# Graph units of an attention block: q/k parts written out and stacked through GpSimd's transfer queue instead of SyncE's

## The reference

```python
nodes = {-1: inputs}
for c in range(6):
    q = ew[c, 0] * (nodes[in_q] @ We[eq] + be[eq])
    k = ew[c, 1] * (nodes[in_k] @ We[ek] + be[ek])
    v = ew[c, 2] * (nodes[in_v] @ We[ev] + be[ev])
    o = _mha(q, k, v, Wq[c], Wk[c], Wv[c], Wo[c])     # 8 heads of width 16, softmax over 1024 keys
    nodes[c] = act_w[c] * o + q
out = layernorm(nodes[5], ln_g, ln_b)
x = x + out
```

## Time and profile before

| what | value |
|---|---|
| runs | 3316.85 us median, 3299.77 to 3317.97 |
| the profiled execution | 3333.32 us, of which the span is 3331.5 us |
| busy | TensorE 90%, VectorE 73%, ScalarE 65%, GpSimd 12% of the span |
| transfers | 245.09 MB, of them 239.85 MB on the queue of SyncE |
| granted clock of TensorE | 0.938 of full speed over the span |
| the graph stage | from about 883 us to about 3286 us |

### The profile page before, as it was taken

One profiled execution on the slowest core, in us unless ns is written; L12 is line 12 of the kernel. 1 busy time (PEld: TensorE's weight loads), 2 busy tenths in 40 slices (PEclk: granted clock), 3 DMA queues, 4 the chain that ended last, 5 costly groups with the idle time before them and its releaser, 6 DMA issues. The chain is left out here.

```text
span 3331.5 us, 49190 instructions
## 1 busy us (share of the span) xinstructions
PE 2998.8 (90%) x19007; PEld 1331.5 (40%) x19007; DVE 2418.4 (73%) x3094; ACT 2151.3 (65%) x2695; POOL 389.8 (12%) x330
## 2 busy tenths in 40 slices
PE   5699989989569999999999999999999999999994
PEld 4355555555323333333333333333333333333331
DVE  6656555554266688888888888888888888888853
ACT  1155555556313477777777777777777777777783
POOL 0000000000100011111111111111111111111114
PEclk9699999999755699999999999999999999999997
DMA  6000000000252244434444344434434444443302
GB/s 169 17 11 4 24 1 27 1 11 11 88 99 50 45 84 107 105 93 103 82 94 100 91 91 100 105 93 102 106 71 103 97 99 85 107 100 94 68 21 84
DMA packets 144224, 245.09 MB, mean 74 GB/s; under 512 B 56482, under 2 KB 92726, under 8 KB 140918
## 3 DMA queue, kind: packets, MB, share of 16 engines
q1 hardware_dynamic: 143414, 239.85, 32.2%
q10 hardware_dynamic: 576, 2.10, 0.2%
HBM read 165.00 MB, written 74.10 MB: 72 GB/s over the span
## 5 line engine op out<-in xcount | busy, mean ns | idle before, releaser
L1436 ACT ACTIVATE pt_b<-ps_max 128x1024 f32<-128x1024 f32 x1516 | 1493.1, 1024 | 436.1 <-PE ps_max L1287 431.8
L1469 DVE TENSOR_REDUCE mx_b<-ps_pair 128x2 f32<-128x1024 f32 (+1 forms) x1032 | 1245.6, 1207 | 243.9 <-PE ps_pair L1273 235.0
L1323 PE MATMUL ps_ctx<-pt_b,vs 128*32 128x512 f32 x6144 | 842.4, 621 | 3.8 <-ACT c_b L1425 3.5
L1469 DVE TENSOR_REDUCE mx_b<-ps_misc 128x1 f32<-128x512 f32 x1032 | 706.9, 685 | 163.9 <-PE ps_misc L1273 145.9
L1287 PE MATMUL ps_max<-qs,ks 50*128 50x512 f32 x3032 | 800.9, 443 | 3.6 <-DMA qs<-mpart 3.0
L1273 PE MATMUL ps_pair<-ks,qs 48*128 48x512 f32 x2040 | 557.7, 479 | 131.8 <-DVE mx_b L1469 104.2
L1287 PEld LDWEIGHTS ps_max<-qs,ks 50*128 50x128 f32 x3032 | 364.9, 190 | 341.0 <-ACT pt_b L1436 246.0
L1273 PE MATMUL ps_misc<-ks,qs 48*128 48x512 f32 x1032 | 482.2, 467 | 7.6 <-DVE mx_b L1469 0.6
L1273 PEld LDWEIGHTS ps_pair<-ks,qs 48*128 48x128 f32 x2040 | 226.9, 192 | 454.8 <-DVE mx_b L1469 395.2
L775 ACT ACTIVATE pt<-ps_max,cb 128x512 f32<-128x512 f32 x342 | 215.4, 684 | 236.0 <-PE ps_max L652 179.9
L1273 PEld LDWEIGHTS ps_misc<-ks,qs 48*128 48x128 f32 x1032 | 199.6, 193 | 360.9 <-DVE mx_b L1469 287.6
(11 more groups left out here) (181 smaller groups left out, 2382.6 us busy)
## 6 DMA issues: line engine op xcount, KB each, us to landing
partd<-part SPq DMA_DIRECT2D x24, 2048.0 KB, 9.1
qs<-partd SPq DMA_DIRECT2D x288, 128.0 KB, 5.7
ks<-partd SPq DMA_DIRECT2D x288, 128.0 KB, 6.7
xq<-node SPq DMA_DIRECT2D x24, 512.0 KB, 3.9
xk<-node SPq DMA_DIRECT2D x24, 512.0 KB, 4.8
xv<-node SPq DMA_DIRECT2D x24, 512.0 KB, 5.5
xf<-node SPq DMA_DIRECT2D x24, 512.0 KB, 4.7
node<-nt_b SPq DMA_DIRECT2D x48, 256.0 KB, 2.2
```

What stands on the lines that cost most here:

```text
L1323: ins = pe.matmul(psO[SLOT * i:SLOT * i + SLOT, :], vs[u % 2][:, kb, QUAD * (s // HALF_STEPS) + i], pt[:, (QUAD * S + i) % ENTRIES], start ...
L1436: act.activation(pt[:, e:e + 2].rearrange("p k n -> p (k n)"), at[:], ACT.Exp, scale=SCALE_B).then_inc(exp_done, 1)
L1469: nc.vector.tensor_reduce(mx2[:, at:at + n], (psP, psX)[p % 2][:, 0:CHUNK * n].rearrange("p (h n) -> p h n", h=n), AX.X, ALU.max).then_inc ...
```

## The change

`spill` and `stack` are moved from SyncE's program to GpSimd's, and are otherwise the same: the same waits, the same sources and destinations, the same 25 transfers for a unit. All other transfers stay with SyncE. In GpSimd's `unit(u)`, `stack(u+1, 1)` stands behind the first maxima split, `spill(u+2)` behind the last split of unit u + 2, and `stack(u+2, 0)` between `normalise(u, 0)` and the next maxima split. At the start, unit 0 is spilled and stacked before the parts of unit 1 are split.

```diff
@@ sync
-                def spill(w):
-                    sp.wait_ge(split_done, PJ * (w + 1))
-                    ...
-                    sp.dma_start(partd, part[:].bitcast(F32)).then_inc(spilled, D16)
-                def stack(w, q):
-                    ...
                     if u:
                         maxima_rows(u, 1)
                         rows_of(NG * u - 1)
-                    if u < LAST:
-                        stack(u + 1, 1)
                     if u:
                         spread(NG * u - 1)
                         store(u - 1, 0)
...
                     load_residual(u)
-                    if u < LAST - 1:
-                        spill(u + 2)
                     if u < LAST:
                         spread(NG * u)
                     if u < LAST:
                         rows_of(NG * u + 1)
-                    if u < LAST - 1:
-                        stack(u + 2, 0)
...
-                spill(0)
-                stack(0, 0)
-                stack(0, 1)
-                spill(1)
                 maxima_rows(0, 0)
-                stack(1, 0)
@@ gpsimd
+                def spill(w):
+
+                    pool.wait_ge(split_done, PJ * (w + 1))
+                    if w:
+                        pool.wait_ge(stacked[0], STACK * w)
+                        pool.wait_ge(stacked[1], STACK * w)
+                    pool.dma_start(partd, part[:].bitcast(F32)).then_inc(spilled, D16)
+
+                def stack(w, q):
+
+                    if w >= 2:
+                        pool.wait_ge(exp_done, exps(w - 2, NS // 2 * (q + 1)))
+                    pool.wait_ge(spilled, D16 * (w + 1))
+                    heads = slice(2 * q, 2 * q + 2)
+                    for t, (a, b) in enumerate(TERMS):
+                        for qk, dst, k in ((0, qs, a), (1, ks, b)):
+                            src = partd[:, qk, k].rearrange("(j r d) t -> r d j t", r=2, d=DV)
+                            for odd in range(2):
+                                at = P // 2 * odd + DV * t
+                                pool.dma_start(dst[w % 2][at:at + DV, heads, :].bitcast(F32),
+                                             src[odd][:, heads]).then_inc(stacked[q], D16)
...
                     if u:
                         split_maxima(u, 1)
+                    if u < LAST:
+                        stack(u + 1, 1)
                     if u < LAST - 1:
                         for n in range(PJ - 1):
                             split(u + 2, n)
...
                         split(u + 2, PJ - 1)
+                        spill(u + 2)
                     if not u:
                         split_maxima(0, 1)
                     normalise(u, 0)
+                    if u < LAST - 1:
+                        stack(u + 2, 0)
                     if u < LAST:
                         split_maxima(u + 1, 0)
...
-                for w in range(2):
-                    for n in range(PJ):
-                        split(w, n)
+                for n in range(PJ):
+                    split(0, n)
+                spill(0)
+                stack(0, 0)
+                stack(0, 1)
+                for n in range(PJ):
+                    split(1, n)
+                spill(1)
                 split_maxima(0, 0)
+                stack(1, 0)
```

More of the change, by code:

```diff
@@ L1127, in load_residual @@
                     sp.dma_start(xf[:], row(node, u)).then_inc(f_in, D16)
-                def spill(w):
-                    sp.wait_ge(split_done, PJ * (w + 1))
-                    if w:
-                        sp.wait_ge(stacked[0], STACK * w)
-                        sp.wait_ge(stacked[1], STACK * w)
-                    sp.dma_start(partd, part[:].bitcast(F32)).then_inc(spilled, D16)
-                def stack(w, q):
[L1139 to L1149, removed]
                 def maxima_rows(w, q):
```

## The result

The changed kernel takes 3643.43 us, the median of four runs (3584.0 to 3667.45), against 3308.31 us for the kernel before on the same occasions. The ratio is 1.0916, with a 95% interval of 1.0758 to 1.1074: 9% slower, where no change was forecast. The profiled execution of the changed kernel took 3650.4 us (3333.32 before), its span is 3648.6 us.

What follows compares the result with a forecast made beforehand. TensorE, busy 90% of the span, was taken as the bound. Only the graph's start gained, 2.3 us, the other terms 0: 3316.85 - 2.3 = 3314.5 us, range 3284 to 3346 us.

Steps and rivals of the forecast that it cites:

- p: Time one stacking transfer's issue holds GpSimd, taken as 1.1 us, between a low end of 0.42 and a high of 2.04.
- the threshold of 1.69 us: At each unit's start, the longest issue time per stacking transfer on GpSimd before the output has to wait.
- the second rival: GpSimd's issues wait for VectorE's running reductions, growing to 2.31 us each: 3486 us, chance 0.04.
- Term 2: Each unit's start: 12 issues delay GpSimd's first split half a microsecond, absorbed; inverses of group 3 land sooner; time 0.
- Term 3: Each unit's middle: GpSimd's stacking and spill delay the maxima split some us, still ahead of need; time 0.
- Term 1: The graph's start: spill and stacking issued by GpSimd let TensorE start at 922.5 instead of 924.83, gain 2.3 us.
- Term 4: SyncE's queue: 25 issues, 10.5 us, leave it per unit; no engine but GpSimd waits for SyncE there; time 0.
- The first: Rival: GpSimd becomes late and the output waits in each of 21 units: 3370 us, 3415 at the high end; chance 0.12.
- The clock's rival: Start shift moves the low clock around unit 0: second low stretch gone, 3285 us, chance 0.07; another added, 3348, chance 0.04.
- a sign that I had named: Near the graph's start: the forecast is wrong if the low clock after 977 us has another length.

Runs made afterwards that it cites:

- f3: The changed kernel with both waits of e1_hold, and at the start stack(1, 0) also waits until unit 0's maxima rows have landed: 3307.86 us.
- e1_hold: The changed kernel, but GpSimd waits until the sums of group 3 (mid-unit, group 1) have landed before issuing the stacking transfers: 3314.91 us.
- e8: The changed kernel with group 3's sums issued by GpSimd, ahead of the stacking in the same queue, with their own semaphore: 3360.3 us.
- e3: The changed kernel with VectorE's reciprocal 13 rounds behind its group instead of 9, transfers unchanged: 3333.81 us.
- e2: The kernel before, all transfers on SyncE, with stack(u+1, 1) put ahead of group 3's sums in SyncE's order: 3704.38 us.
- e6: Only stack(w, 0), the 12 mid-unit transfers, moved to GpSimd's queue; spills and the other half stay with SyncE: 3371.05 us.

## Why the prediction was wrong

**Where it was right.** No transfer of `partd` is waited for in the steady units. GpSimd did not become late: with p = 0.50 us, the threshold of 1.69 us is far off, and the issue does not get longer beside VectorE's reductions (its minimum and its median are both 500 ns), so the second rival has nothing behind it either. The Trainium skill (SBUF — State Buffer, Who interferes with whom, the practical consequences) excepts a `tensor_reduce` on trn2 from such a block, and the trace agrees. From the Trainium skill (DMA: Bandwidth & Descriptors, Latency and other measured facts) I had worked out an estimate of 0.8 us for p; the measured 0.50 decides. In Term 2 the first split was not delayed at all. Term 3 held for what it counted: TensorE waited for maxima rows once, at the start. It did not count the sums of group 1, which land in 10.4 us beside the middle pile.

**Term 1, mis-sized.** TensorE started at 923.9 and not at 922.5; the gain is 0.9 us, not 2.3. The issue was cheaper, but the spill needed 11.4 us from its issue at 897.79 to the first stacking at 909.19, where I had 8.7. TensorE then waited 7.1 us instead of 3.0 for the maxima rows of unit 0, the same crowding as below, which I did not have (with the rows ahead of the stacking, in f3, it is 3.1).

**The step that failed is Term 4, with the second half of Term 2.** I wrote: "No engine waits for SyncE in the steady units except GpSimd, which has room. Time: 0." I had read the list of waits and found none of VectorE for SyncE's transfers, but a wait that does not appear can have little room. VectorE came to the reciprocal at 2013.36, and the sums, issued from 2006.47, needed 3.6 us: 3.3 us of room. Before:

```profile
2006.47 2.49 SPq L1165 DMA_DIRECT2D den_b<-c_b  x4
2009.06 0.99 SPq L1148 DMA_DIRECT2D qs<-partd  x2
```

In the kernel before they were covered by an order that I had described and not priced: on SyncE's one queue the sums stood ahead of the stacking. With two queues, nothing keeps them ahead. GpSimd starts stacking at 2001.95, 2.5 us before the sums go out, and they need 11.0 us. I counted for the small transfers only what a queue without the pile gives (`invd` does land in 1.6 us now where it took 8.7) and not what sharing the engines with the pile takes.

**The price of a stall.** Even with that wait seen, I would have written 21 x 3 = 63 us, 2% of the time. In the 21 units TensorE's idle time grew from 81.5 to 162.1 us, by 81, and the units by 326. I held the clock for a matter of the start alone. Yet my own rows had a sign of it: the start's idle stretch had a granted clock of 0.50, and unit 0 took about twice a unit's time behind it. The Trainium skill (TensorE: Matmul & The Clock Gate, HAM oscillation — how this bites in real kernels) describes it: a wait that comes back in each tile brings the half rate back in each tile. The 21 units here agree, with shorter waits than it tells of.

**The rivals.** The first had the right shape, a transfer's side effect paid once a unit in 21 units, and the wrong engine, queue and price. Its 3370 us, and even its far end of 3415, lie below what was measured. The clock's rival came true in this one execution: the second low stretch is missing, the granted clock is 1.00 from 1082 to 1160, and the first output comes 17.9 us earlier, not 30. It was a sign that I had named, and it is small beside the loss.

## What to carry to other kernels

When a transfer is moved to another queue, list every small transfer that stood ahead of it in the old queue, and the room that each consumer had, also where no wait shows. Moving large transfers out of the way of a queue does not move them out of the way of the engines: hold them until the small ones have landed (e1_hold), or send the small ones first in the same queue (e8), or have their consumer come for them later (e3). And where TensorE is the bound at full clock, price a stall that comes back in each unit with the clock behind it: 1.4 to 3 us of stall cost 8 to 16 us here.

## What the runs showed of the hardware that was not expected

- A transfer of 32 pieces of 4 KB holds GpSimd for 0.50 us (SyncE 0.42), and one of 2 MB for 0.62 us.
- The cost of a stall is steep at its foot: 1.39 us of VectorE's time cost 9.5 us for each unit and 2.73 us cost 14.7, while e2's wait of 7.35 us cost 17.2. Waits of 1.1 us on average in the middle of a unit (e6) cost 1.5.
- The same stall cost 7.7 us in the middle of a unit and 14.7 at its start.
